# Max products of the attention issued between the experts of a mixture layer

## The reference, cut to what matters

```
attn = einsum('bhnd,bhmd->bhnm', q, k) * scale        # 8 heads of 8, 1024 x 1024 scores
attn = softmax(attn); out = einsum('bhnm,bhmd->bhnd', attn, v)
...
gate_scores = x @ Wg + bg;  mask = one_hot(top_k(gate_scores, 2)).sum(-2)
h = gelu(einsum('td,edh->teh', x, W1) + b1)           # all 8 experts, hidden 128
y = einsum('teh,ehd->ted', h, W2) + b2;  out = einsum('ted,te->td', y, mask)
```

## Time and profile before

| what | us |
|---|---|
| median of 3 runs (4240.89 to 4246.01) | 4241.19 |
| the profiled execution | 4239.35 |
| its span in the profile | 4237.5 |
| TensorE busy | 3920.9 |
| VectorE busy | 2902.9 |
| ScalarE busy | 2728.1 |
| GpSimd busy | 859.5 |

### The profile page before, as it was taken

How to read it: one execution, slowest core, us unless ns; L and a number is a source line. 1 busy time by engine, 2 the same in 40 slices (tenths; PEclk the granted TensorE clock), 3 DMA queues, 4 the chain that set the end, 5 groups by cost and what they waited for, 6 DMA issues and landing times.

```text
span 4237.5 us, 61596 instructions
## 1 busy us (share of the span) xinstructions
PE 3920.9 (93%) x21509; PEld 1301.7 (31%) x21509; DVE 2902.9 (69%) x4956; ACT 2728.1 (64%) x4896; POOL 859.5 (20%) x1263
## 2 busy tenths in 40 slices
PE   5988999999999999999999999999999999999796
PEld 3222323233332323323232332323333232332222
DVE  3866757677675766857677675767867677686571
ACT  0555767667676666767667676666767667676474
POOL 4122212121121312212121211312212131220211
PEclk7899999999999999999999999999999999999898
DMA  5213211222122122212222121122211212210100
GB/s 102 36 25 56 37 29 31 41 48 41 29 39 41 31 41 49 38 22 31 52 37 41 35 38 35 31 41 48 41 24 32 53 31 41 42 28 19 31 1 6
DMA packets 115606, 156.30 MB, mean 37 GB/s; under 512 B 21391, under 2 KB 63119, under 8 KB 115261
## 3 DMA queue, kind: packets, MB, share of 16 engines
q1 hardware_dynamic: 115297, 152.36, 20.5%
HBM read 120.01 MB, written 29.36 MB: 35 GB/s over the span
## 4 chain that ended last, share of the span: by engine, by line
PE 66%; ACT 10%; DVE 8%; issue 7%; POOL 3%; DMA 2%; SPq 1%; POOLq 0%; ACTq 0%; DVEq 0%
PE acc L866 17%; PE st L852 17%; PE nat L832 15%; DVE tile_max L1252 5%; PE side L799 3%; ACT hidden L1027 2%; ACT prob L1056 2%; PE side L696 2%; PE side L673 2%; PE side L785 2%; PE side L753 1%; DMA k_rows<-k_scratch 1%; ACT hidden L972 1%; DVE ln_s L1157 1%; POOL centred L1340 1%
## 5 line engine op out<-in xcount | busy, mean ns | idle before, releaser
L1252 DVE TENSOR_REDUCE tile_max<-nat 128x1 f32<-128x512 f32 x4096 | 2598.6, 684 | 1170.3 <-PE nat L832 1150.1
L1056 ACT ACTIVATE prob<-st 128x512 f32<-128x512 f32 x4096 | 2298.1, 596 | 1362.5 <-PE st L852 1309.6
L852 PE MATMUL st<-q_rows,k_rows 99*128 99x512 bf16 x4096 | 1572.8, 384 | 65.2 <-ACT prob L1056 55.7
L832 PE MATMUL nat<-k_rows,q_rows 96*128 96x512 bf16 x4096 | 1449.7, 386 | 88.9 <-DMA k_rows<-k_scratch 41.6
L866 PE MATMUL acc<-prob,v_padded 128*32 128x512 f32 x8192 | 1096.6, 607 | 1.0 <-ACT prob L1056 1.0
L852 PEld LDWEIGHTS st<-q_rows,k_rows 99*128 99x128 bf16 x4096 | 398.3, 97 | 1312.2 <-ACT prob L1056 1030.7
L832 PEld LDWEIGHTS nat<-k_rows,q_rows 96*128 96x128 bf16 x4096 | 402.0, 98 | 629.2 <-DVE tile_max L1252 346.7
L1412 POOL TENSOR_SCALAR max_parts<-neg_max 128x16 bf16<-128x16 f32 x128 | 26.3, 206 | 1685.5 <-DVE neg_max L1259 1205.4
L866 PEld LDWEIGHTS acc<-prob,v_padded 128*32 128x32 f32 x8192 | 161.4, 108 | 338.4 <-issue 276.9
L1337 POOL TENSOR_SCALAR ln_s<-ln_s 128x8 f32<-128x8 f32 x64 | 13.0, 203 | 986.5 <-DVE ln_s L1157 986.5
L799 PE MATMUL side<-hidden,w 128*64 128x512 f32 x512 | 136.5, 616 | 0.0
(11 more groups left out here) (129 smaller groups left out, 2105.8 us busy)
## 6 DMA issues: line engine op xcount, KB each, us to landing
q_rows<-q_scratch SPq DMA_DIRECT2D x288, 128.0 KB
k_rows<-k_scratch SPq DMA_DIRECT2D x96, 384.0 KB
x_rows<-in_x SPq DMA_DIRECT2D x62, 512.0 KB, 6.7
q_scratch<-hidden SPq DMA_DIRECT2D x32, 384.0 KB
k_scratch<-hidden SPq DMA_DIRECT2D x96, 128.0 KB
group_weights<-in_routed SPq DMA_DIRECT2D x64, 129.0 KB, 2.1
q_rows<-max_rows SPq DMA_DIRECT2D x512, 3.0 KB
out_h<-out_rows SPq DMA_DIRECT2D x16, 256.0 KB, 2.1
```

The lines of the kernel that those rows point to most:

```text
L832: eng.matmul(NAT[place % len(NAT)][:, :], QA[u][0:K_NAT, h, c:c + P], KA[u][0:K_NAT, h, kh * 512:kh * 512 + 512], start=True, stop=True)\
L852: eng.matmul(ST[n % 2][:, :], KA[u][0:K_ALL, h, t * P:t * P + P], QA[u][0:K_ALL, h, half * 512:half * 512 + 512], start=True, stop=True)\
L1056: eng.activation(prob[:, n % TILES, :], ST[n % 2][:, :], ACT.Exp).then_inc(exp_done, 1)
L1252: eng.tensor_reduce(mx[:, q % 2, j // 8, j % 8 // 2, j % 2:j % 2 + 1], NAT[place % len(NAT)][:, :], AX.X, ALU.max).then_inc(nat_free, 1)
```

## The change

Seven max products go between the experts of FW. In a phase's slot 48 `max_tiles` gives the seven tiles 94 to 100 instead of one, and TensorE issues one after each of the experts 0 to 6. From then on it is six tiles ahead of its usual place, and gives that up one by one: slots 51, 54, 57, 60, 63 and 66, which hold FY0 to FY5, have no max product. The turn, tied to the tile number, moves from slot 55 to slot 49, the fold on VectorE and the split on GpSimd from slot 49 to 48, and the DMA of the maxima from slot 55 to 49. The serial end, which has a sixteenth FW, is unchanged.

```diff
+AHEAD = 6
+def max_tiles(side, n):
+    def extra(m):
+        for slot in range(m, max(m - 3 * AHEAD, -1), -1):
+            if any(x[0] == "FW" for x in side.get(slot, ())):
+                return AHEAD - (m - slot) // 3
+        return 0
+    return range(n + SUPER + LEAD + (extra(n - 1) if n else 0), n + SUPER + LEAD + extra(n) + 1)
...
                 elif name == "FW":
...
                         for par, half in enumerate(HALVES):
                             eng.matmul(both[par][:, :], MS[half, e, :], MTb[half, :], start=False, stop=True)\
                                 .then_inc(fw_ready, 1)
+                        for where in between[e:e + 1]:
+                            nat(*where)
...
+                    tiles = max_tiles(side, n)
+                    between = [(kind, it, n0, m) for m in tiles] if len(tiles) > 1 else []
                     for k, stage in enumerate(side[n]):
-                        side_stage(stage, found[n, k], n0 + n, n)
-                    ahead = n + SUPER + LEAD
-                    q = ahead // SUPER
-                    if ahead % SUPER == TURN and (kind != "last" or q <= SUPERS):
-                        turn(n0, q, last=(kind == "last" and q == SUPERS))
+                        side_stage(stage, found[n, k], n0 + n, n, between)
+                    for m in tiles:
+                        if m % SUPER == TURN and (kind != "last" or m // SUPER <= SUPERS):
+                            turn(n0, m // SUPER, last=(kind == "last" and m // SUPER == SUPERS))
...
-                    if kind != "last" or q < SUPERS:
-                        nat(kind, it, n0, ahead)
+                    for m in tiles[len(between):]:
+                        if kind != "last" or m < ATTN:
+                            nat(kind, it, n0, m)
```

More of the change, by code:

```diff
@@ L628, in body @@
                 for n in range(n_tiles(kind)):
-                    ahead = n + SUPER + LEAD
-                    if ahead % SUPER == TURN:
+                    for ahead in max_tiles(side, n):
                         q = ahead // SUPER - 1
-                        if kind != "last" or q < SUPERS:
+                        if ahead % SUPER == TURN and (kind != "last" or q < SUPERS):
                             max_dma(kind, it, n0, q, last=(kind == "last" and q == SUPERS - 1))
@@ L682, in tok_block, with side_stage @@
                 return mm
-            def side_stage(stage, n, tile, slot):
+            def side_stage(stage, n, tile, slot, between=()):
                 name, b, k, is_last, *more = stage
@@ L1279, in body @@
                         ins.then_inc(s_late, 1)
[L1280 to L1287, removed]
+                    for m in max_tiles(side, n):
+                        q = m // SUPER
+                        if m % SUPER == TURN and (kind != "last" or q <= SUPERS):
+                            rows_out(n0, q, last=(kind == "last" and q == SUPERS))
+                        if kind != "last" or q < SUPERS:
+                            reduce_tile(n0, m)
+                            if m % SUPER == SUPER - 1:
+                                super_max(n0, q)
                     for k, stage in enumerate(side[n]):
@@ L1429, in body @@
                         eng.wait_ge(s_rest, N_SET[s_rest])
[L1430 to L1433, removed]
+                    for m in max_tiles(side, n):
+                        if m % SUPER == SUPER - 1 and (kind != "last" or m < ATTN):
+                            split_max(n0, m // SUPER)
                     for k, stage in enumerate(side[n]):
```

## The result

The changed kernel took 4252.08 us (median of 11 runs, 4246.77 to 4260.24) against 4241.19 us before (11 runs, 4237.21 to 4247.83): ratio 1.0024, 95% interval 1.0015 to 1.0033. I had forecast 4246.6 us, +0.13%, no change that can be told with a lean to slower: the forecast of 1.0013 lies just outside this interval. The truth lies near the edge of what I had called "no change".

The account below looks back on a forecast made before the run. FW was bound by TensorE and ScalarE close to balance, the stretch to FY6 by full TensorE. +1.35 - 0.99 = +0.36 us a batch, x 15 = +5.4 us on the 4241.19 median: 4246.6 us, range 4231 to 4256.

Parts of the forecast that it names:

- Which engine bounds which stretch: Expert 0 to third `st`: TensorE and ScalarE close to balance, with idle TensorE time; from there to FY6: TensorE full.
- The price of a product in FW: Between experts, an inserted max product costs 0.41 us, with 0.10 for each change of form; +1.35 us a batch.
- the first two products are free: Behind experts 0 and 1, max products cost nothing, since expert 2 waits for the table load and first Gelus.
- Slots 48 and 49: Two max products leave, one and the turn come, before a 0.59 us wait for `prob`: cost 0, at most 0.25.
- The emptied slots: Slots 51 to 66, third `st` to FY6: six max products and the turn leave, 18.78 us against 19.77, -0.99 us.
- The floor I took at 1.10 us: Slots 51 to 66: two banks keep `st` of n + 2 at least 1.10 us behind `st` of n.
- three causes in one term: FY1 to FY2: 0.52 us gained from one product, the turn, and the wait for a `nat` bank behind the turn.
- rival 3: Slots 57 to 62: the exponentials' floor takes the gain, leaving 0.5 us a batch; +12.8 us, 4254.0 us; chance 0.17.
- free changes of form: Between experts, changes of form cost nothing, each product 0.22 us; -9.3 us, 4231.9 us, faster by 0.22%; chance 0.16.
- a cost only on the way in: Between experts, only the way into the 64-row form costs; +0.87 - 0.99 a batch, -1.8 us, 4239.4 us; chance 0.11.
- step 3: Slots 51 to 66: six max products and the turn leave the stretch where TensorE is full; -0.99 us a batch.
- max products that don't come early in effect: In FW, a bank or semaphore holds the first max product until FW is over; no size given, chance almost nothing.

Follow-up runs that it names:

- pairs: Changed kernel with max products two by two behind experts 1, 3, 5 and one behind expert 7; expert 0 to third `st` 15.81 us, one run.
- half_rows: Changed kernel with the seven early max products reading 64 of 96 rows; expert 0 to third `st` 15.48 us, one run.
- one_51: Changed kernel with only two early max products, behind experts 0 and 1, and only slot 51 emptied; third `st` to FY6 19.76 us, one run.
- gather_83: Changed kernel with early products behind experts 0 (one), 1 (three), 7 (three); slots 57, 60, 69, 72, 82, 83 emptied; ratio to before 0.9924.
- the second comparison: The changed kernel run again, without edit, beside the kernel before; ratio 1.0016 (1.0007 to 1.0025).
- gather_late: Changed kernel with early products behind experts 0 (one), 1 (three), 7 (three); slots 54, 57, 60, 66, 69, 72 emptied; ratio to before 0.9943.

## Why the prediction was right, and where it was off

- **Which engine bounds which stretch** was right: the same products cost 1.44 us in the balanced stretch and gave 1.00 in the one where TensorE was full.
- **The price of a product in FW** (0.41 forecast) was right in kind and up to 0.02 short: the pitch is 1.59 or 1.60, not 1.58, since each of the two borders takes 0.31 or 0.32. From expert 2 to expert 7 it takes 7.98 us instead of 6.57, which is 1.41 of the 1.44; the forecast had 1.35. `pairs` and `half_rows` show that it is the change of the array's form; by which of the two ways above, they don't. That the first two products are free was right (`one_51`).
- **Slots 48 and 49** cost nothing, as forecast: the third `st` still waited 0.46 us for `prob`.
- **The emptied slots**: -0.99 forecast, -1.00 measured, and the split by slot held for 51 (nothing), 57 and 60 (0.22 each, 0.47 forecast for both), 63 and 66 (nothing). The floor I took at 1.10 us measures 1.08 where it binds (`st` at 1071.80 and, next but one, 1072.88). In the stretch of slot 54 the sum was right, but I had named three causes in one term; the runs put 0.47 to 0.48 of the 0.53 measured to the turn's place, and a turn one slot earlier is enough for it. The max product of slot 54 gave nothing: `gather_83` has it back, and FY1 to FY2 takes 2.42 there against 2.41.
- **The sum**: +0.36 forecast a batch, +0.44 measured (+1.44 and -1.00), so +6.6 us and not +5.4 by the stretches. The rest of the first ratio is inside its interval, and no run accounts for it. With 6.6 us the kernel stands close to the 0.2% (8.5 us) that I drew between "same" and "slower"; the first comparison fell just beyond it, the second just inside. By its time alone the first comparison, 4252.08 us, lay nearer to rival 3 (4254.0) than to the forecast (4246.6); only the stretches and the second comparison speak for the forecast.
- **The rivals**: free changes of form (-9.3 us) fell with `pairs`; a cost only on the way in (-1.8 us) fell with the 0.31 from mask to max product; the floor that leaves only 0.5 of step 3 (+12.8 us) fell with slots 57 and 60, which gave theirs; max products that don't come early in effect fell with VectorE's reductions inside FW.
- **What I overlooked**: I compared the idle TensorE time of FW with the products as a sum and did not ask for the other order. The wide waits are before expert 2 and behind expert 7; there seven products are free.

Not settled: whether the part of a border's 0.10 on either side is the same when the next product is float32 and when it is bf16; no run separates them. Nor is it settled whether that 0.10 is a drain of the array or a weight load that comes late.

## What to carry to other kernels

A product moved into an idle gap pays what its neighbours make it pay. Before filling a gap, take the start-to-start time of both borders from the trace, and put like products together in the widest wait instead of one in each narrow one. On the other side, look in each slot from which work is taken for the second wait (here a two-bank ring at 1.10 us): four of the six emptied slots (51, 54, 63 and 66) gave nothing, and two at a quite different place (behind the output stage, where VectorE was late) gave the most, 0.59 us a batch together.

## What the runs showed of the hardware that I had not expected

- A 64-row product placed behind two 64-row mask products lets the next expert start 0.11 us later, in half the time of its own 0.22 (before expert 3 even 0.01 later, 1060.12 to 1060.13): it runs partly beside work on the other half of the rows. With a product of 96 rows the two borders in the same place take 0.31 and 0.32.
- The weight load of a max product starts 0.21 us ahead of its product within one form of the array, and less than 0.01 ahead behind a change of form.
- The time before the first FW varies between profiled executions, from 541.95 us (before) to 552.03 (`gather_late`), with no order by kernel, while the stretches in the batches come again within 0.02. The changed kernel alone has spans of 4244.9 and 4257.6. So spans of single profiles (4237.5 before against 4244.9) say less on this change than two stretches of 15 us.
